# Routing placed between a group's layer-norm statistics and its normalisation on VectorE, in the projection stage

## The reference, cut to what matters

```python
# end of the scan stage: y are the scan's outputs, 256 features a token
return y @ Wout + b_out + res
...
x = x + _L0_attn_ref(_layernorm(x, axis=-1), ...)
x = x + _L0_ffn_ref(_layernorm(x, axis=-1), ...)
...
def _layernorm(x, axis=-1, eps=1e-05):
    m = jnp.mean(x, axis=axis, keepdims=True)
    v = jnp.var(x, axis=axis, keepdims=True)
    return (x - m) / jnp.sqrt(v + eps)
...
# in _L0_ffn_ref: the routing weights
logits = jnp.einsum('bsh,he->bse', hidden_states.astype(jnp.float32), router_w)
affinity = jax.nn.sigmoid(logits)
top_scores, top_idx = jax.lax.top_k(affinity, K)          # K = 8 of 64
top_w = top_scores / (jnp.sum(top_scores, axis=-1, keepdims=True) + 1e-09)
```

## Time and profile before

| | |
|---|---|
| median of 3 runs | 2330.77 us (2330.49 to 2334.44) |
| the profiled execution's own time | 2336.39 us |
| its span, first to last instruction | 2334.7 us |
| busy: PE, DVE, ACT, POOL | 1848.8, 1405.6, 998.7, 891.1 us |
| mean granted TensorE clock, as a share of 2.4 GHz | 0.844 |
| `project`, from its first matmul to the next block's first instruction | 350.06 to 461.93 us |

### The profile page before, as it was taken

How to read it: one execution, slowest core, us unless ns; L and a number is a source line. 1 busy time by engine, 2 the same in 40 slices (tenths; PEclk the granted TensorE clock), 3 DMA queues, 4 the chain that set the end, 5 groups by cost and what they waited for, 6 DMA issues and landing times. The chain is left out here.

```text
span 2334.7 us, 28969 instructions
## 1 busy us (share of the span) xinstructions
PE 1848.8 (79%) x8208; PEld 1433.9 (61%) x8208; DVE 1405.6 (60%) x3320; ACT 998.7 (43%) x1840; POOL 891.1 (38%) x795
## 2 busy tenths in 40 slices
PE   8999996479999999997577657767689984443699
PEld 7999993257777777775455435545466652222487
DVE  6412224467666666665457657757665558997566
ACT  5302012145445554543455435524377762222454
POOL 5601101035555555554000035510068873221265
PEclk9899587689999999998567678879889996665799
DMA  2001000176545555543000045410011101000455
GB/s 61 2 1 20 1 1 7 25 161 146 115 108 108 116 106 120 108 108 68 19 1 1 2 91 108 90 36 1 1 46 38 43 18 27 1 1 1 82 120 123
DMA packets 114094, 129.92 MB, mean 56 GB/s; under 512 B 40262, under 2 KB 58826, under 8 KB 114026
## 3 DMA queue, kind: packets, MB, share of 16 engines
q1 hardware_dynamic: 112216, 128.65, 25.9%
q10 hardware_dynamic: 1810, 0.42, 0.1%
HBM read 125.51 MB, written 3.54 MB: 55 GB/s over the span
## 5 line engine op out<-in xcount | busy, mean ns | idle before, releaser
L800 POOL TENSOR_TENSOR ffn_alo<-ffn_a,ffn_ahi 128x512 fp32r<-128x512 f32 x520 | 670.5, 1292 | 507.8 <-ACT ffn_ahi L761 504.1
L827 DVE TENSOR_TENSOR ffn_a<-ffn_G,ffn_mask 128x512 f32<-128x512 f32 x384 | 264.7, 689 | 238.1 <-ACT ffn_G L769 216.7
L769 ACT ACTIVATE ffn_G<-ffn_G 128x512 f32<-128x512 f32 x384 | 223.5, 582 | 355.6 <-PE ffn_G L116 353.3
L761 ACT ACTIVATE ffn_ahi<-ffn_a 128x512 fp32r<-128x512 f32 x520 | 324.6, 624 | 32.4 <-DVE ffn_a L831 29.0
L114 PE MATMUL ypsum<-ffn_ahi,ffn_hi 128*128 128x512 f32 x520 | 227.7, 438 | 51.3 <-POOL ffn_alo L800 37.0
L114 PE MATMUL ffn_G<-xn_hi,ffn_hi 128*128 (+1 forms) x520 | 220.3, 424 | 29.9 <-DVE ffn_lo L807 27.1
L831 DVE TENSOR_TENSOR ffn_a<-ffn_U,ffn_a 128x512 f32<-128x512 f32 x320 | 221.4, 692 | 30.1 <-DVE ffn_a L827 1.0
L115 PE MATMUL ffn_G<-xn_lo,ffn_hi 128*128 (+1 forms) x520 | 214.6, 413 | 0.0
L116 PE MATMUL ffn_G<-xn_hi,ffn_lo 128*128 (+1 forms) x520 | 214.3, 412 | 0.0
L115 PE MATMUL ypsum<-ffn_alo,ffn_hi 128*128 128x512 f32 x520 | 209.8, 404 | 0.0
L116 PE MATMUL ypsum<-ffn_ahi,ffn_lo 128*128 128x512 f32 x520 | 208.9, 402 | 0.0
(11 more groups left out here) (551 smaller groups left out, 3709.9 us busy)
## 6 DMA issues: line engine op xcount, KB each, us to landing
ffn_mask<-mask_rows_top SPq DMA_DIRECT2D x128, 512.0 KB, 6.9
ffn_mask<-mask_rows_top SPq DMA_DIRECT2D x16, 1024.0 KB, 8.3
ffn_mask<-mask_rows_zone SPq DMA_DIRECT2D x16, 1024.0 KB, 8.3
ffn_mask<-mask_rows_steps SPq DMA_DIRECT2D x16, 512.0 KB, 4.9
x<-in_L_attn_x SPq DMA_DIRECT2D x8, 256.0 KB, 4.8
ffn_raw<-in_L_ffn_expert_gate_k SPq DMA_DIRECT2D x16, 128.0 KB, 4.0
ffn_raw<-in_L_ffn_expert_up_k SPq DMA_DIRECT2D x16, 128.0 KB, 4.1
ffn_raw<-in_L_ffn_expert_down_k SPq DMA_DIRECT2D x16, 128.0 KB, 4.4
```

The lines of the kernel that those rows point to most:

```text
L761: act.activation(ahi[i][:, :], a[i][:, :], ACT.Copy).then_inc(k.ahi_done, 1)
L769: act.activation(gate if masked(c) else a[c % RING_A][:, :], gate, how, **kw).then_inc(k.r_done, 1)
L800: eng.tensor_tensor(alo[i][:, :], a[i][:, :], ahi[i][:, :].bitcast(F32), ALU.subtract).then_inc(k.alo_done, 1)
L827: dve.tensor_tensor(out, gate[:, :], mask(c), ALU.mult).then_inc(k.t_done, 1)
```

## The change

DVE's turn in `project` is written in another order. Before, the group's residual, statistics and normalisation stand together (step 2), then the routing of the preceding group (step 13), then `xn_lo` (step 6). Now the residual and the statistics stand first (20 to 23), then the routing (13), then the two halves of the normalisation (24, 25) and `xn_lo` (6). The order on the other engines is the same.

The two one-column memsets of `post_norm_part` write to a tile of their own, `tick_norm`, since the routing writes `tick` too. This holds for every stage that uses `post_norm_part`; they stay as many and as small.

```diff
@@ -74,6 +74,7 @@
     k.tick2 = k.sb("tick_gpsimd", [P, 1])
+    k.tick_norm = k.sb("tick_norm", [P, 1])
@@ -167,7 +168,7 @@
     if part == 0:
         dve.wait_ge(k.x_done, n + 1)
-        dve.memset(k.tick[:, :], 0.0)
+        dve.memset(k.tick_norm[:, :], 0.0)
@@ -2611,9 +2612,9 @@
                 def body(p):
-                    p.part(0, post, 2)
+                    p.part(0, post, 20, 21, 22, 23)
                     p.part(1, post, 13)
-                    p.part(0, post, 6)
+                    p.part(0, post, 24, 25, 6)
```

## The result

The change made the kernel slower: 2345.31 us median (2339.18 to 2352.25, 19 runs) against 2336.84 us (2326.42 to 2345.62, 19 runs), a ratio of 1.0038 with a 95% interval of 1.0023 to 1.0053. By the ratio that is +8.9 us with an interval of 5.4 to 12.4 us (the medians lie 8.5 us apart). The forecast was +11.0 us.

What follows compares the result with a forecast made beforehand. The late affinity was taken to bound the `project` loop. Turn costs of 7.52 + 2.31 + 1.74 - 0.60 = +10.97 us on the 2330.77 median gave 2341.7 us, range 2335 to 2347.

Steps and rivals of the forecast that it cites:

- What bounds the loop: In `project`, the routing waits for its affinity, which comes last, behind `output` and the copies of y and logits.
- The fixed cost: From the routing's end to the next logits: 3.77 us instead of 1.89, +1.88 a turn; seven turns sum to +10.97 us.
- the `xn_lo` side: Behind the routing, `xn_lo` ends about 3.55 us after the routing's end, before the logits' start at 3.77.
- I keep its mean: `output` in `project` was assumed to keep its mean of 3.04 us over six turns, despite TensorE's uncertain clock.
- The low end of the clock: In `project`, transposes at full clock give 4.4 us less, `output` at 2.40 another 3.9 less: total +2.7, or 2333.5.
- the same rival: In `project`, transposes and `output` mostly at full clock soften the loss: 2333.5 us, or half way 2335; chance 12%.
- The third rival: In `project`, a harder clock: every `output` at 3.62 us, 3.5 us more, total 2345.2; chance 15%.
- The strict reading: In `project`, PE's longer idle piece, some 4.5 us, would leave more of the next `output` at 1.2 GHz.
- The signs: In `project`: turns 13.7 to 15 us, seventh about 11.4; affinity waits 2.4 to 3.6; routing's end to logits 3.6 to 3.8.
- One sign of being wrong: In a turn of `project`, an affinity arriving earlier than 7 us after the logits would count against the prediction.
- The seventh turn: Last changed turn of `project`, without `output`: routing starts 2.48 us earlier and fills the hole, -0.60 us; about 11.4 us long.
- the first: Routing fills the GpSimd hole in every turn of `project`: 11.38 us a turn, 79.7 against 87.3, total 2323.2; chance 3%.

Runs made afterwards that it cites:

- Experiment 3: Kernel before plus the new tile, DVE's old order, with logits' transpose ahead of `output` on PE, their copy and sigmoid ahead of y's copy on ACT: ratio 0.9986.
- experiment 4: Changed kernel with the logits' transpose ahead of `output` on PE, their copy and the sigmoid ahead of y's copy on ACT: ratio 0.9958 to the kernel before.
- experiments 5 to 7: Changed kernel with, separately, routing weights ahead of normalised tokens on PE and ACT, a 0.48 us DVE memset, one of about 0.95 us: ratios 1.0014, 1.0051, 1.0083.
- second set: The changed kernel timed and profiled again with no edit, against the kernel before: ratio 1.0045 (1.0030 to 1.0059), project 118.60 us.
- experiment 1: Kernel before with only the new tile `tick_norm`, DVE's order as it was: ratio 1.0005 (0.9984 to 1.0026), project 111.03 us.
- experiment 5: Changed kernel with the routing weights' transpose ahead of the normalised tokens' on PE, their copy ahead of `xn_hi` on ACT: ratio 1.0014, project 120.90 us.
- stall_half: Changed kernel with one 128x512 memset (0.48 us) on DVE between routing and normalisation: ratio 1.0051 to the kernel before, project 123.09 us.
- experiment 7: Changed kernel with one 128x1024 memset (about 0.95 us) on DVE between routing and normalisation: ratio 1.0083 to the kernel before, project 128.68 us.

## Why the prediction was right, and where it was off

**What bounds the loop: right.** The affinity was the last thing to come. Experiment 3 shows it by bringing it early; experiment 4 shows that with it early the very same change gains.

**The fixed cost: right to 0.1 us in the sum.** Turn length less `output`, before and after, for the seven turns: +1.76, +2.37, +1.93, +1.83, +1.93, +1.92 and -0.65, together +11.1 us, against the predicted 4 x 1.88, 2.31 (second turn), 1.74 (fourth) and -0.60 (seventh), together +10.97. The routing's end to the logits took 3.82 us instead of 3.77. One step was wrong inside it: the `xn_lo` side was to end first by some 0.1 us, and with the 0.17 us that it needs behind `xn_hi` it ends at the same time.

**The clock: the mis-sized term.** "I keep its mean", 3.04 us of `output` a turn, was the step that failed; it measured 13.76 / 6 = 2.29. The low end of the clock had 2.40 for it (3.9 us less), so the profile's 4.5 us went slightly beyond that end, while the transposes, which the same rival wanted fast, stayed at 1.11 and 1.06. The third rival, a harder clock through longer idle of PE, went the wrong way, though the idle piece came as computed (4.48 us). The Trainium skill, TensorE: Matmul & The Clock Gate, section "What's actually happening", says activity releases the throttle; the trace agrees that the clock rises in `output` and is low again for the transposes behind the idle piece (1.11 us, as in the earlier trace rows). The strict reading that I took from it, a longer slow part of the next `output`, isn't what the traces show. I had taken the length of the turn for something that has no say in the clock; experiments 5 to 7 show that it has. In the changed loop the turn without `output`, 11.40 us, and 2.25 of `output` make the 13.65 at which the clock's rises came. In the loop before, from the second turn on, at most 9.58 and at most 3.62 make 13.2, so it could not settle there.

**The signs.** Most came: the wait for GpSimd is gone, the transposes start 1.08 us after the routing with PE idle for 4.48, the seventh turn took 11.33. Three missed narrowly, and two of these by the clock: turns 2 to 6 took 13.6 us instead of 13.7 or more, DVE's idle time ahead of the routing was 2.2 us in the third turn instead of at least 2.4, and the routing's end to the logits was 3.82 instead of at most 3.8. One sign of being wrong came too: in the third turn the affinity was there 6.8 us after the logits (398.05 less 391.25), and the bound named was 7. It was badly chosen. Before, with `output` at 2.40, the fourth turn already had 6.99, so a fast `output` alone brings it about, without any change in what bounds the loop.

**The number: in part luck.** The forecast was 2341.7 us and the median 2345.31, within the range of 2335 to 2347. But the forecast stood on three runs of before with a median of 2330.77, and over 19 runs it was 2336.84. With that start the same +10.97 gives 2347.8, above the range. A change that came out smaller than forecast and a start that came out higher offset each other.

**The seventh turn: right.** 11.33 us for 11.38; the routing started at 450.34, behind the aggregation, with GpSimd's work under it.

**Outside the stage.** The prediction expected no change there. The span less project is 2222.9 us before and 2231.4 after, but 2224.1 in the second profile of the same changed kernel, and in all ten profiles, whose code outside project is the same but for the tile, it lies between 2222.6 and 2231.4. So of the first profile's 15.1 us 6.6 lie in the stage, and the other 8.5 lie outside it, where this profile is the longest of the ten and the second one of the same code is 7.3 shorter. The timed +8.9 us (5.4 to 12.4) agrees with both the 6.6 of project and the predicted 11.0. In the second set 1.0045 is 7.0 to 13.8 us, which just leaves 6.6 out; but project varies too, since under the old order it took 111.84 us in one profile and 111.03 in the other (experiment 1), so that the growth is 6.6 to 7.6 by the four profiles. Whether anything above that is more than scatter stays open.

Of the rivals, the first did not happen here, but its sum was a fair forecast for the kernel with the early logits: 11.38 us a turn and -7.6 us, measured 10.8 to 11.4 and -10.0 in project. It had to be asked what would make its condition true, and the answer was two lines in PE's and ACT's order.

## What to carry to other kernels

An idle hole on an engine can be filled only by work whose input is already there: before looking at the hole's size, look at when that input arrives, and at what is queued behind the moved wait on the other engines. If the input's lateness is itself a matter of order, as here a small copy that stood behind a large matmul's result, repair that first; then the move that lost 6.6 us gains 5.2.

## What the runs showed of the hardware

The rises of the granted clock from 1.2 to 2.4 GHz came 13.65 us apart in the settled turns of the changed loop. Two stretches of its profile, one in the third turn and one in the fourth, show it (all engines, as in 5):

```profile
393.85:394.45 0.60, 0.60 (x2) 0.18 (x1) 0.58 (x1) 0.00 (x0) 0.00 (x0) 0.73 0.00 0
...
407.50:408.10 0.60, 0.60 (x2) 0.19 (x1) 0.60 (x1) 0.00 (x0) 0.00 (x0) 0.73 0.00 0
```

The same mean in both puts the rise at the same place in both, and they start 13.65 us apart. In experiment 5 the distance was the same while the turns took 14.02 and 13.83 us. A loop near that length can be drawn to it. If it is too long, `output` starts later against the rise and has less of its work at 1.2 GHz; the work that it no longer does at 1.2 GHz takes half the time at 2.4, so the excess about halves each turn (1.32, 0.71, 0.37, 0.18, 0.10 in experiment 5; 1.72, 1.00, 0.48, 0.26 in `stall_half`). If it is too short, `output` grows: 2.17, 2.21, 2.23, 2.25 in turns 2 to 5 of the changed kernel.

It isn't always drawn: turns of 14.12 us (experiment 5) and 13.93 us (`stall_half`) were followed by 14.97 and 15.37, with the rises 17.1 us apart, and in the kernel before two rises stood 10.2 apart (393.2 and 403.4). What decides between these distances no run here shows.

In the profiles, a turn without `output` that was 0.05 us shorter (experiment 5) bought nothing, and one that was 0.88 us longer (experiment 7) cost 10.1 / 7 = 1.4 a turn. In such a loop a small change can't be read off a turn's length; the turn less `output` shows it, as 11.35 against 11.40 did here.
